# A four-block transformer on one core: head sums of the first attention as products of high and low parts

## The chip, the core and the metric

One core of a Trainium2 chip runs the whole network. The metric is the device time of one execution in microseconds. TensorE multiplies, VectorE, ScalarE and GpSimd work elementwise, SyncE issues the transfers. Each engine runs its own instructions in order; semaphores order them across engines.

## The reference

The input is x, 16 sequences of 256 tokens of 128 features. Four blocks follow, each with a residual: a gated linear attention, an expert FFN, a softmax attention, the FFN again. The change lies in the first:

```python
# phi_q, phi_k: elu(rope(.)) + 1; beta: decay; mix: softmax over the M = 2 memories; 32 heads, D = 4
K = K * bt[..., None] + pk[:, :, None, :]
S = S * bt[..., None, None] + pk[:, :, None, :, None] * vt[:, :, None, None, :]
num = jnp.einsum('bhd,bhmdc->bhmc', pq, S)
den = jnp.einsum('bhd,bhmd->bhm', pq, K) + EPS
y = jnp.sum(num / den[..., None] * mt[..., None], axis=2)
```

For each memory m, head and value component c (0 to 3), num is the sum over d of pq[d] · S[m][d, c].

## The kernel before, in words

The tokens are worked in NT = 8 tiles of 512 (two sequences), features on the partitions. `S[:, m, c, :]` holds, for memory m, 128 rows (d, head) by 512 tokens; c = 4 is the denominator. VectorE makes these ten rows per tile with scans (`scan`, L1619), then multiplies those of m = 0 with phi_q (`product`, L1626, in pieces of 512 and 1024 columns); GpSimd multiplies those of m = 1 (`product`, L755, five of 512 columns). TensorE sums over d with 128 × 128 tables of ones and zeros (`numerator`, L1171), four products in full precision (F32) per m, accumulating in bank 7 or 6; the four denominator sums are in `denominators` (L1181). VectorE makes the weights (L1694 to L1701), TensorE spreads them (`weights`, L1192), ScalarE copies them (L963), VectorE multiplies them with the numerators (`weighted`, L1603), GpSimd adds the two memories (L780), and TensorE projects (`project_y`, L1199 and L1203) in the next tile's first step.

Elsewhere an f32 product is replaced by three of type F32R (`split_product`, L343 to L345), whose operands are a rounded high part, made by a copy into an F32R tile on ScalarE, and a low part, the difference, made by a subtraction.

The order is written by hand. Stage t runs `CH` = 32 steps c. In each step of a stage with an FFN tile beside it (f = t − 2, so stages 2 to 9) stands one FFN unit: on TensorE gate, up and down, three products each; on ScalarE silu (L542) and the high part of the hidden row before (L552); on VectorE the gating product (L582), which reads PSUM, and, in odd steps, the low part (L558); on GpSimd the low part (L558) in even steps. TensorE's up of unit c waits for the L582 of unit c − 2 and its gate for silu of c − 2; down of c − 3 waits for that unit's low part. Behind the unit, each engine's `attn(t, c)` issues what of the attention belongs to step c. In stages 0 and 1 no FFN stands beside, and only the waits set the pace. Stage 2 also makes the high and low parts of all FFN weights: L466 on ScalarE, L471 on GpSimd. In stage t, steps 11 to 16 hold key products (L1609) and the scans of m = 0; 17 and 19 VectorE's products; 18 and 20 to 23 the scans of m = 1; 19 and 21 to 24 GpSimd's products; 20 and 22 the numerators of m = 0; 24 and 25 those of m = 1; 24 and 25 the weights; 28 and 29 the weighted products; 30 their sum.

After the first ten stages come the second attention and the second FFN.

Of the kernel before, what the change touches and what calls it, by code (L numbers as in the profile page):

```python
# [16 lines left out]
F32 = mybir.dt.float32  # L17
# [126 lines left out]
def program(nc, a_x, a_Wq, a_Wk, a_Wv, a_Wbeta, a_bbeta, a_Wmix, a_bmix, a_Wout, a_bout, a_ln_g, a_ln_b,  # L144
            b_Wq, b_bq, b_Wk, b_bk, b_Wv, b_bv, b_Wo, b_bo, f_Wg, f_Wu, f_Wd, consts, out):
    ctx = ExitStack()
    with ctx:  # L147
# [34 lines left out]
        ident = cst("ident")  # L182
        SELR = sb("SELR", [P, 2 * NJ + 3, P], F32R)
        MASKB = sb("MASKB", [P, 3, P], BF16)
        ONES = sb("ONES", [P, P])
# [30 lines left out]
        ARENA = sb("ARENA", [P, 20736])  # L216
        ARENA_R = sb("ARENA_R", [P, 20224], F32R)
        at = {F32: 0, F32R: 0}

        def take(*shape, dt=F32):  # L220
# [64 lines left out]
        XAH = take(TOK, dt=F32R)  # L285
        XAL = take(TOK, dt=F32R)
        at[F32R] = 0

# [15 lines left out]
        ld = sems("ld", "x0 x1 x tables_a tables_b wa wb ba bb")  # L304
        pr = sems("prep", "wt wtc la ones selr wb wout ba bmix bqkr bqk zero")
# [3 lines left out]
        A = sems("a", "u_k u_q ex_k ex_q re_k re_q phi_k phi_q clip scaled beta scan prod0 prod1 num0 num1 den dp rc "  # L309
                      "wgt rep rs ay y z zsum zg zb done")  # L310
# [4 lines left out]
        BPROJ = ["q", "qs", "k", "ks"]  # L315
        b_ready = {n: sem(f"b_{n}_ready") for n in BPROJ}
        b_used = {n: sem(f"b_{n}_used") for n in BPROJ}
        B = sems("b", "u_q u_k hi lo v_ready v_used st_ready st_used kst_ready kst_used row_ready row_used nmh nml "
# [88 lines left out]

        def f_source(n):
# [316 lines left out]
        def _(g):  # L725
# [31 lines left out]
            def attn(t, c):  # L757
                old, nxt = t - 1, t + 1
                if is_tile(t):
# [171 lines left out]
        def _(act):  # L931
# [22 lines left out]
            def half_tanh(t, m):  # L954
# [186 lines left out]
        def _(pe):  # L1141
# [65 lines left out]
            def attn(t, c):  # L1207
# [61 lines left out]
                if is_tile(t):  # L1269
                    if c == 20:  # L1270
                        pe.wait_ge(a_used["v3"], t + 1)
                        numerator(t, 0, (0, 1))
                    if c == 22:
                        numerator(t, 0, (2, 3))
                        pe.wait_ge(a_used["v2"], t + 1)
                        denominators(t)
                    if c == 24:
                        pe.wait_ge(n_a.lo, min(t + 2, NT))
                        after(pe, n_f.lo, t)
                        numerator(t, 1, (0, 1))  # L1280
                    if c == 25:
                        numerator(t, 1, (2, 3))
                    if c == 26:
                        weights(t, 0)
                    if c == 27:
                        weights(t, 1)
# [3 lines left out]
            def project_b(nxt, i):  # L1290

                pe.wait_ge(n_b.lo, NT + nxt.n + 1)
                if i:
                    pe.wait_ge(b_used[BPROJ[i - 1]], nxt.n + 1)
                split_product(pe, bank[6], WBH[:, i, :], WBL[:, i, :], XH[:, :],
                              XL[:, :]).then_inc(b_ready[BPROJ[i]], 1)

            def project_v(nxt, subs):

                pe.wait_ge(b_used[BPROJ[-1]], nxt.n + 1)  # L1300
                if 0 in subs:
# [52 lines left out]
            pe.wait_ge(pr.bqkr, 5)  # L1354
            pe.wait_ge(pr.selr, 1)
            pe.wait_ge(pr.ba, 2)
            for t in range(-1, NT + 2):
# [104 lines left out]
            def slot(t, b):  # L1462
# [3 lines left out]
                for k in range(UNITS):  # L1466
# [16 lines left out]
                    if k == T_LAG - 1 and has1:  # L1483
# [3 lines left out]
                        if b == 1 and nxt.real():  # L1487
                            pe.wait_ge(b_used[BPROJ[-1]], nxt.n + 1)
                        stack2(n - 1, op, 1 - b, 0)
# [55 lines left out]
        def _(v):  # L1545
# [83 lines left out]
            def attn(t, c):  # L1629
# [56 lines left out]
                if is_tile(t):  # L1686
# [10 lines left out]
                    if c == 25:  # L1697
# [3 lines left out]
                        v.scalar_tensor_tensor(WGT[:, :], MIX[:, :], 1.0, RC[:, :], ALU.add,  # L1701
                                               ALU.mult).then_inc(A.wgt, 1)
                    if c == 28:
                        weighted(t, 0)
                    if c == 29:
                        weighted(t, 1)

            def rope_b(t, k, name, table, dst, bias):
                v.wait_ge(b_ready[name], t.n + 1)
                after(v, (B.u_q, B.u_k)[k], t.n)  # L1710
                v.scalar_tensor_tensor(seqs(dst), seqs(bank[6]), bias, spread(cst(table), SPT), ALU.add,
                                       ALU.mult).then_inc(b_used[name], 1)

# [193 lines left out]
```

## Time and profile before

| | us |
|---|---|
| median of 3 runs | 1718.75 (1716.77 to 1719.26) |
| the profiled execution | 1717.04 |
| its span | 1715.2 |
| busy: TensorE / VectorE / ScalarE / GpSimd | 1613.6 / 1075.4 / 1014.2 / 888.1 |

A busy time says how much an engine did in the whole span, not where it set the pace, and it holds the time in which an instruction that has started is held up inside. A timeline row is one instruction or a few merged ones with start and duration; the idle time before it and what ended that stand in brackets. A matmul row's duration holds its pipeline's depth; the distance from start to start is what TensorE spends on it. A full-precision product leaves two records.

### The profile page before, as it was taken

To read this page: it belongs to the slowest core of one execution; us is meant where nothing else is said; L and a number is where in the kernel's file an instruction comes from. 1 tells how busy PE (TensorE), PEld (TensorE's weight loads), DVE (VectorE), ACT (ScalarE), POOL (GpSimd) and SP (SyncE) were. 2 spreads that over 40 slices of the span, in tenths; PEclk is the share of its full clock that TensorE was granted. 3 is DMA by queue.
4 is the path that set the end of the run, shared out by engine and by line. 5 is a ranking of instruction groups with operands and counts; after the bars stand their busy time and mean duration, and the time that the engine had idled before them with its cause. 6 is when DMAs were issued, how large, how long until landed. Compare 5 with 4: busy or idle time off the path is not lost. (4 is left out here: it accounts for less than half of the span.)

```text
span 1715.2 us, 24775 instructions
## 1 busy us (share of the span) xinstructions
PE 1613.6 (94%) x7232; PEld 1247.1 (73%) x7232; DVE 1075.4 (63%) x1871; ACT 1014.2 (59%) x1872; POOL 888.1 (52%) x793
## 2 busy tenths in 40 slices
PE   3678999999999999999999999988999999999998
PEld 2356677878787878886666666656888888888887
DVE  5667778686869595557666666643454554554544
ACT  2237464646464646555887878875555555555554
POOL 3669764646454544362777777773333333333322
PEclk9789999999999999999999999998999999999999
DMA  3035543444443435541000000012555555555554
GB/s 106 1 111 184 189 138 132 143 142 148 148 148 128 148 130 184 205 177 57 1 1 1 2 0 1 1 38 99 187 193 203 201 187 190 197 193 205 194 187 135
DMA packets 72548, 215.88 MB, mean 126 GB/s; under 512 B 7387, under 2 KB 20832, under 8 KB 72416
## 3 DMA queue, kind: packets, MB, share of 16 engines
q1 hardware_dynamic: 72416, 214.35, 36.1%
q8 instruction: 55, 0.90, 0.2%
q14 instruction: 77, 0.63, 0.1%
HBM read 199.64 MB, written 14.68 MB: 125 GB/s over the span
## 5 line engine op out<-in xcount | busy, mean ns | idle before, releaser
L558 POOL TENSOR_TENSOR ARENA_R<-ARENA,ARENA_R 128x512 fp32r<-128x512 f32 x256 | 344.1, 1344 | 600.3 <-ACT ARENA_R L552 599.5
L582 DVE TENSOR_TENSOR ARENA<-ARENA,pair 128x512 f32<-128x512 f32 x512 | 349.1, 682 | 449.0 <-PE pair L345 410.4
L542 ACT ACTIVATE ARENA<-bank 128x512 f32<-128x512 f32 x512 | 306.1, 598 | 464.8 <-PE bank L345 463.0
L343 PE MATMUL pair<-ARENA_R 128*128 128x512 f32 x1064 | 417.1, 392 | 10.6 <-DVE ARENA L582 5.0
L345 PE MATMUL pair<-ARENA_R 128*128 128x512 f32 x1064 | 414.7, 390 | 0.0
L344 PE MATMUL pair<-ARENA_R 128*128 128x512 f32 x1064 | 414.2, 389 | 0.0
L552 ACT ACTIVATE ARENA_R<-ARENA 128x512 fp32r<-128x512 f32 x512 | 319.9, 625 | 36.1 <-DVE ARENA L582 33.6
L913 POOL TENSOR_TENSOR ARENA_R<-ARENA,ARENA_R 128x512 fp32r<-128x512 f32 x192 | 249.2, 1312 | 80.0 <-ACT ARENA L1120 76.6
L343 PE MATMUL bank<-ARENA_R 128*128 128x512 f32 x568 | 239.8, 422 | 23.0 <-DVE ARENA L1609 17.7
L343 PEld LDWEIGHTS pair<-ARENA_R 128*128 128x128 f32 x1064 | 200.7, 189 | 60.2 <-issue 7.3
L345 PEld LDWEIGHTS pair<-ARENA_R 128*128 128x128 f32 x1064 | 200.8, 189 | 42.4
L344 PEld LDWEIGHTS pair<-ARENA_R 128*128 128x128 f32 x1064 | 200.9, 189 | 41.3
L344 PE MATMUL bank<-ARENA_R 128*128 128x512 f32 x568 | 223.6, 394 | 0.0
L345 PE MATMUL bank<-ARENA_R 128*128 128x512 f32 x568 | 223.5, 393 | 0.0
L558 DVE TENSOR_TENSOR ARENA_R<-ARENA,ARENA_R 128x512 fp32r<-128x512 f32 x256 | 195.4, 763 | 0.1
L1781 DVE TENSOR_REDUCE ARENA<-bank 128x2 f32<-128x512 f32 (+1 forms) x192 | 130.8, 688 | 76.2 <-PE bank L1379 43.8
L343 PEld LDWEIGHTS bank<-ARENA_R 128*128 128x128 f32 x568 | 108.1, 190 | 52.0 <-DVE ARENA L1609 21.4
L1415 PE MATMUL pair<-ARENA_R 128*128 128x512 f32 x384 | 135.2, 433 | 8.5 <-ACT ARENA L1096 6.9
L1120 ACT ACTIVATE ARENA_R<-pair 128x512 fp32r<-128x512 f32 x192 | 115.8, 603 | 34.0 <-PE pair L1403 25.7
L344 PEld LDWEIGHTS bank<-ARENA_R 128*128 128x128 f32 x568 | 108.3, 191 | 23.5 <-issue 4.3
L345 PEld LDWEIGHTS bank<-ARENA_R 128*128 128x128 f32 x568 | 107.9, 190 | 23.3
L1619 DVE TENSOR_TENSOR_SCAN ARENA<-ARENA 128x512 f32<-128x512 f32 x80 | 121.4, 1525 | 0.0
(216 smaller groups left out, 2027.1 us busy)
## 6 DMA issues: line engine op xcount, KB each, us to landing
ARENA_R<-split_weights SPq DMA_DIRECT2D x360, 512.0 KB, 4.7
split_weights<-ARENA_R SPq DMA_DIRECT2D x24, 512.0 KB, 3.9
X<-in_L_attn_a_x_dram SPq DMA_DIRECT2D x8, 256.0 KB, 5.4
ARENA<-in_L_ffn_Wg_dram SPq DMA_DIRECT2D x8, 256.0 KB, 2.9
ARENA<-in_L_ffn_Wu_dram SPq DMA_DIRECT2D x8, 256.0 KB, 3.4
ARENA<-in_L_ffn_Wd_dram SPq DMA_DIRECT2D x8, 256.0 KB, 3.9
out_dram<-X SPq DMA_DIRECT2D x8, 256.0 KB, 4.2
CST<-in_tables_dram SPq DMA_DIRECT2D x1, 835.5 KB, 4.6
```

What stands on the lines that cost most here:

```text
L343: pe.matmul(dst, wh, xh, start=start, stop=False)
L344: pe.matmul(dst, wh, xl, start=False, stop=False)
L345: return pe.matmul(dst, wl, xh, start=False, stop=stop)
L542: act.activation(SG[:, c % 2, :], bank[c % 2], ACT.Silu).then_inc(F.sil, 1)
L552: act.activation(HH[:, G % FC, :], HF[:, G % FC, :], ACT.Copy).then_inc(F.hh, 1)
L558: eng.tensor_tensor(HL[:, G % FC, :], HF[:, G % FC, :], HH[:, G % FC, :].bitcast(F32), ALU.subtract).then_inc(lo_done(G)[0], 1)
L582: v.tensor_tensor(HF[:, c % FC, :], SG[:, c % 2, :], bank[2 + c % 2], ALU.mult).then_inc(F.mul, 1)
L913: g.tensor_tensor(PL[:, u % RING, :], PT[:, u % RING, :], PH[:, u % RING, :].bitcast(F32), ALU.subtract).then_inc(B.pl, 1)
L1120: act.activation(dst[:, u % RING, :], bank[2 + u % 2], ACT.Exp, scale=DB ** -0.5).then_inc(B.t_used, 1)
L1415: m = pe.matmul(bank[4 + qb], VS[:, p, 2 * ob + kb, at:at + P], (PH, PL)[i][:, u % RING, :], start=(u < 2 and i == 0), stop=(g == NG - 1 a ...
L1619: v.tensor_tensor_scan(S[:, m, c, :], BETA[:, m, :], KV[:, c, :], 0.0, ALU.mult, ALU.add).then_inc(A.scan, 1)
L1781: v.tensor_reduce(dst, src, AX.X, ALU.max, negate=True).then_inc(B.row_used, 1)
```

## The change

The four products per m of `numerator` become eight: each `S[:, m, c, :]` is split into a high part `NUH` (ScalarE, two components at once) and a low part `NUL` (for m = 0 on GpSimd, for m = 1 on VectorE), and both are multiplied with a rounded copy `SUMR` of the sum tables, which GpSimd makes at the start. Steps move: numerators to 21 and 23 (m = 0), 26 and 28 (m = 1), the second weighted product to 30, the sum to 31. The eight semaphores of the second attention's four projections become two counters, `b_ready` and `b_used`; the waits name the same events. The core of the diff:

```diff
         ARENA_R = sb("ARENA_R", [P, 20480], F32R)        # was 20224
+        NUH = take(2, 2, TOK, dt=F32R)
+        NUL = take(2, 2, TOK, dt=F32R)
...
+        def product_lo(eng, t, m, p):
+            eng.wait_ge(A.nuh, 4 * t + 2 * m + p + 1)
+            if m == 0:
+                after(eng, A.num1, t)
+            else:
+                eng.wait_ge(A.num0, t + 1)
+            for i in range(2):
+                eng.tensor_tensor(NUL[:, p, i, :], S[:, m, 2 * p + i, :], NUH[:, p, i, :].bitcast(F32),
+                                  ALU.subtract).then_inc(A.nul, 1)
...  GpSimd, start
+            g.wait_ge(ld.tables_a, 16)
+            for c in range(DA):
+                g.tensor_copy(SUMR[:, c, :], cst(f"sum_{c}")).then_inc(pr.sumr, 1)
             a_rstd(g, 0)
...  GpSimd, step
                     if c in (19, 21, 22, 23, 24):
                         product(t, (19, 21, 22, 23, 24).index(c))
-                    if c == 30:
+                    if c in (19, 21):
+                        product_lo(g, t, 0, (c - 19) // 2)
+                    if c == 31:
                         g.wait_ge(A.ay, 2 * (t + 1))
...
             def rotated(nxt, i):
                 name = "qk"[i]
-                after(g, b_used[name], nxt.n + 1)
-                after(g, b_used[name + "s"], nxt.n + 1)
+                after(g, *projected(b_used, nxt, name + "s"))
...  ScalarE
+            def product_hi(t, m, p):
+                if m == 0:
+                    act.wait_ge(A.prod0, 3 * t + 2 + p)
+                    after(act, A.num1, t)
+                else:
+                    act.wait_ge(A.prod1, 5 * t + 3 + 2 * p)
+                    act.wait_ge(A.num0, t + 1)
+                act.activation(NUH[:, p, :, :], S[:, m, 2 * p:2 * p + 2, :], ACT.Copy).then_inc(A.nuh, 1)
...
+                    if c in (18, 20):
+                        product_hi(t, 0, (c - 18) // 2)
+                    if c in (24, 26):
+                        product_hi(t, 1, (c - 24) // 2)
...  TensorE
-            def numerator(t, m, comps):
-                for c in comps:
-                    pe.wait_ge(*((A.prod0, 3 * t + 2 + c // 2) if m == 0 else (A.prod1, 5 * t + 2 + c)))
-                    x = pe.matmul(bank[(7, 6)[m]], cst(f"sum_{c}"), S[:, m, c, :], start=(c == 0), stop=(c == DA - 1))
-                if DA - 1 in comps:
+            def numerator(t, m, p):
+                pe.wait_ge(A.nul, 8 * t + 4 * m + 2 * p + 2)
+                for i in range(2):
+                    for part in (NUH, NUL):
+                        x = pe.matmul(bank[(7, 6)[m]], SUMR[:, 2 * p + i, :], part[:, p, i, :],
+                                      start=(p + i == 0 and part is NUH), stop=(p + i == 2 and part is NUL))
+                if p:
                     x.then_inc((A.num0, A.num1)[m], 1)
...  steps: numerator(t, 0, 0) at c == 21, (t, 0, 1) at 23, (t, 1, 0) at 26 ahead of weights(t, 0), (t, 1, 1) at 28
...  VectorE
+                    if c == 25:
+                        product_lo(v, t, 1, 0)
+                    if c == 27:
+                        product_lo(v, t, 1, 1)
                     if c == 28:
                         weighted(t, 0)
-                    if c == 29:
+                    if c == 30:
                         weighted(t, 1)
```

## Rows read from the trace of the kernel before

**Rows 1.** The page: busy us, share of the span and instructions of each engine.
```profile
PE 1613.6 (94%) x7232; PEld 1247.1 (73%) x7232; DVE 1075.4 (63%) x1871; ACT 1014.2 (59%) x1872; POOL 888.1 (52%) x793
```

**Rows 2.** Four stretches: busy us (instructions) by engine, clock, DMA.
```profile
core 0: us, PE busy (x) PEld busy (x) DVE busy (x) ACT busy (x) POOL busy (x), PEclk, DMA share, GB/s
42.00:62.00 20.00, 14.88 (x35) 7.30 (x36) 14.48 (x13) 1.19 (x2) 12.15 (x6) 0.82 0.00 1
172.00:200.00 28.00, 25.60 (x95) 17.61 (x96) 25.19 (x23) 12.98 (x24) 24.24 (x15) 1.00 0.45 158
329.20:375.10 45.90, 44.16 (x183) 33.24 (x182) 45.83 (x58) 24.38 (x46) 24.09 (x21) 1.00 0.41 138
375.40:390.50 15.10, 14.79 (x66) 11.96 (x65) 7.87 (x12) 8.10 (x15) 5.11 (x4) 1.00 0.47 164
```

**Rows 3.** VectorE's timeline: start, duration; in brackets idle time and releaser.
```profile
329.18 0.69 DVE L582 TENSOR_TENSOR ARENA<-ARENA,pair 128x512 f32<-128x512 f32 x1 [4.57 <-ACT ARENA L542]
375.40 0.69 DVE L582 TENSOR_TENSOR ARENA<-ARENA,pair 128x512 f32<-128x512 f32 x1 [0.29 <-PE pair L345]
...
641.86 0.69 DVE L582 TENSOR_TENSOR ARENA<-ARENA,pair 128x512 f32<-128x512 f32 x1 [0.28 <-PE pair L345]
```

**Rows 4.** TensorE's timeline, steps 20 and 26 of tile 4.
```profile
353.38 0.47 PE L343 MATMUL pair<-ARENA_R 128*128 128x512 f32 x1 [0.47 <-DVE ARENA L582]
...
375.88 1.02 PE L1192 MATMUL pair<-ARENA,CST 128*128 128x256 f32 x4
```

**Rows 5.** VectorE's timeline in steps 17 to 21 of tile 4.
```profile
349.73 2.92 DVE L1626 TENSOR_TENSOR ARENA<-ARENA 128x512 f32<-128x512 f32 x2
...
354.30 0.66 DVE L582 TENSOR_TENSOR ARENA<-ARENA,pair 128x512 f32<-128x512 f32 x1
354.87 1.41 DVE L558 TENSOR_TENSOR ARENA_R<-ARENA,ARENA_R 128x512 fp32r<-128x512 f32 x1
356.20 2.30 DVE L1626 TENSOR_TENSOR ARENA<-ARENA 128x1024 f32<-128x1024 f32 x1
...
359.02 1.21 DVE L1619 TENSOR_TENSOR_SCAN ARENA<-ARENA 128x512 f32<-128x512 f32 x1
...
362.07 2.28 DVE L1619 TENSOR_TENSOR_SCAN ARENA<-ARENA 128x512 f32<-128x512 f32 x1
```

**Rows 6.** GpSimd's timeline in steps 19, 20 and 24.
```profile
354.45 1.28 POOL L755 TENSOR_TENSOR ARENA<-ARENA 128x512 f32<-128x512 f32 x1 [2.90 <-DVE ARENA L1619]
355.69 1.73 POOL L558 TENSOR_TENSOR ARENA_R<-ARENA,ARENA_R 128x512 fp32r<-128x512 f32 x1
...
371.01 1.29 POOL L755 TENSOR_TENSOR ARENA<-ARENA 128x512 f32<-128x512 f32 x1 [1.16 <-DVE ARENA L1619]
```

**Rows 7.** L558 by line (min/median/max ns), and L1626 in tile 0.
```profile
L558 DVE TENSOR_TENSOR ARENA_R<-ARENA,ARENA_R x256: 675/685/1458, 116.9 to 1707.3; 128x512 fp32r<-128x512 f32 x128
...
43.84 1.20 DVE L1626 TENSOR_TENSOR ARENA<-ARENA 128x1024 f32<-128x1024 f32 x1
```

**Rows 8.** TensorE's timeline around the first numerator of tile 4.
```profile
354.85 1.88 PE L1171 MATMUL bank<-ARENA,CST 128*128 128x512 f32 x4
...
356.80 0.40 PE L344 MATMUL bank<-ARENA_R 128*128 128x512 f32 x1
```

**Rows 9.** Lines by form: ScalarE's copies of 1024 columns.
```profile
L1035 ACT ACTIVATE ARENA_R<-CST 128x1024 fp32r<-128x1024 f32 x2 | 2.1, 1050 | 0.0
```

**Rows 10.** Timeline of tile 0: GpSimd's products, VectorE's second weighted product.
```profile
44.01 10.89 POOL L755 TENSOR_TENSOR ARENA<-ARENA 128x512 f32<-128x512 f32 x5 [10.86 <-DVE ARENA L1619]
...
59.42 0.69 DVE L1603 TENSOR_TENSOR ARENA<-ARENA,bank 128x512 f32<-128x512 f32 x1 [1.13 <-ACT ARENA L963]
```

**Rows 11.** Timeline of the start, and GpSimd's copies by form.
```profile
8.60 0.69 PE L1151 MATMUL bank<-CST,ARENA 128*128 128x128 f32 x2 [8.60 <-DMA CST<-in_tables_dram]
...
10.74 0.23 POOL L368 TENSOR_SCALAR VE<-MV 128x4 f32<-128x4 f32 x1 [9.28 <-DVE MV L360]
...
L823 POOL CAST SELR<-ARENA 128x128 fp32r<-128x128 f32 x4 | 1.2, 293 | 0.0
```

More of the change, by code:

```diff
@@ L183, in program @@
         SELR = sb("SELR", [P, 2 * NJ + 3, P], F32R)
+        SUMR = sb("SUMR", [P, DA, P], F32R)
         MASKB = sb("MASKB", [P, 3, P], BF16)
@@ L216, in program @@
         ARENA = sb("ARENA", [P, 20736])
-        ARENA_R = sb("ARENA_R", [P, 20224], F32R)
+        ARENA_R = sb("ARENA_R", [P, 20480], F32R)
         at = {F32: 0, F32R: 0}
@@ L304, in program @@
         ld = sems("ld", "x0 x1 x tables_a tables_b wa wb ba bb")
-        pr = sems("prep", "wt wtc la ones selr wb wout ba bmix bqkr bqk zero")
+        pr = sems("prep", "wt wtc la ones selr wb wout ba bmix bqkr bqk zero sumr")
         PROJ = ["k", "ks", "b0", "b1", "q", "qs", "mx", "v0", "v1", "v2", "v3"]
@@ L308, in program @@
         a_used = {n: sem(f"a_{n}_used") for n in PROJ}
-        A = sems("a", "u_k u_q ex_k ex_q re_k re_q phi_k phi_q clip scaled beta scan prod0 prod1 num0 num1 den dp rc "
+        A = sems("a", "u_k u_q ex_k ex_q re_k re_q phi_k phi_q clip scaled beta scan prod0 prod1 nuh nul num0 num1 den dp rc "
                       "wgt rep rs ay y z zsum zg zb done")
@@ L315, in program, with projected @@
         BPROJ = ["q", "qs", "k", "ks"]
-        b_ready = {n: sem(f"b_{n}_ready") for n in BPROJ}
-        b_used = {n: sem(f"b_{n}_used") for n in BPROJ}
+        b_ready, b_used = sem("b_proj_ready"), sem("b_proj_used")
+        def projected(sm, t, name):
+            return sm, len(BPROJ) * t.n + BPROJ.index(name) + 1
         B = sems("b", "u_q u_k hi lo v_ready v_used st_ready st_used kst_ready kst_used row_ready row_used nmh nml "
@@ L1269, in attn @@
                 if is_tile(t):
-                    if c == 20:
+                    if c == 21:
                         pe.wait_ge(a_used["v3"], t + 1)
-                        numerator(t, 0, (0, 1))
+                        numerator(t, 0, 0)
                     if c == 22:
-                        numerator(t, 0, (2, 3))
                         pe.wait_ge(a_used["v2"], t + 1)
                         denominators(t)
-                    if c == 24:
+                    if c == 23:
+                        numerator(t, 0, 1)
+                    if c == 26:
                         pe.wait_ge(n_a.lo, min(t + 2, NT))
                         after(pe, n_f.lo, t)
[L1280 to L1283, printed above, removed]
+                        numerator(t, 1, 0)
                         weights(t, 0)
+                    if c == 28:
+                        numerator(t, 1, 1)
                     if c == 27:
@@ L1293, in project_b @@
                 if i:
-                    pe.wait_ge(b_used[BPROJ[i - 1]], nxt.n + 1)
+                    pe.wait_ge(*projected(b_used, nxt, BPROJ[i - 1]))
                 split_product(pe, bank[6], WBH[:, i, :], WBL[:, i, :], XH[:, :],
-                              XL[:, :]).then_inc(b_ready[BPROJ[i]], 1)
+                              XL[:, :]).then_inc(b_ready, 1)
             def project_v(nxt, subs):
-                pe.wait_ge(b_used[BPROJ[-1]], nxt.n + 1)
+                pe.wait_ge(*projected(b_used, nxt, BPROJ[-1]))
                 if 0 in subs:
@@ L1355, in _ @@
             pe.wait_ge(pr.selr, 1)
+            pe.wait_ge(pr.sumr, DA)
             pe.wait_ge(pr.ba, 2)
@@ L1487, in slot @@
                         if b == 1 and nxt.real():
-                            pe.wait_ge(b_used[BPROJ[-1]], nxt.n + 1)
+                            pe.wait_ge(*projected(b_used, nxt, BPROJ[-1]))
                         stack2(n - 1, op, 1 - b, 0)
@@ L1702, in attn @@
                                                ALU.mult).then_inc(A.wgt, 1)
+                    if c == 25:
+                        product_lo(v, t, 1, 0)
+                    if c == 27:
+                        product_lo(v, t, 1, 1)
                     if c == 28:
                         weighted(t, 0)
-                    if c == 29:
+                    if c == 30:
                         weighted(t, 1)
             def rope_b(t, k, name, table, dst, bias):
-                v.wait_ge(b_ready[name], t.n + 1)
+                v.wait_ge(*projected(b_ready, t, name))
                 after(v, (B.u_q, B.u_k)[k], t.n)
                 v.scalar_tensor_tensor(seqs(dst), seqs(bank[6]), bias, spread(cst(table), SPT), ALU.add,
-                                       ALU.mult).then_inc(b_used[name], 1)
+                                       ALU.mult).then_inc(b_used, 1)
             def split_b(nxt, i):
```

## The prediction

> **What bounds the kernel now.** I read the page first: TensorE is busy 94% of the span [rows 1], which invites a sum made on TensorE alone. So I next took the stretches of the first 650 us, where the first attention runs, and then each engine's own timeline in one of them. From tile 3 on the stages are copies of each other, 88.8 us apart: the L582 of step c = 26 starts at 375.40 in tile 4 and at 641.86 in tile 7, three stages on [rows 3]. I work in tile 4. From its step c = 9 (329.2) to c = 26 (375.1) TensorE is busy 44.16 of 45.90 us, but VectorE is busy 45.83 of 45.90 [rows 2]: after it waited 4.57 us for ScalarE at 329.18 it does not stand idle until 375.40, and then only 0.29 us [rows 3]. Two engines are full there. TensorE may run two FFN units ahead of VectorE's gating product L582 and no further; at 353.38 it hit that limit [rows 4]. After c = 26 TensorE alone is full: 14.79 of 15.10 us, VectorE 7.87 [rows 2].
>
> VectorE is full partly with waiting. Its products with two SBUF inputs and GpSimd's take turns. L755 on GpSimd starts at 354.45 and ends at 355.73; VectorE's L558 starts at 354.87 and takes 1.41 instead of its usual 0.68, so it ends 0.6 after GpSimd does. GpSimd's next one starts at 355.69 and takes 1.73 instead of 1.28; VectorE's L1626 of 1024 columns starts at 356.20 and takes 2.30 instead of 1.20; the scan at 362.07 takes 2.28, the one at 359.02 takes 1.21 [rows 5 to 7]. The L582 at 354.30, which reads PSUM, keeps its 0.66 under the same GpSimd product. As pitches (start to start, since neighbours overlap by some 0.08) I use: GpSimd product 1.25, VectorE product 0.60, scan 1.13, L1626 1.13, PSUM product 0.58.
>
> The rule for this stands in the Trainium skill, SBUF — State Buffer, section "Who interferes with whom": a VectorE instruction with two SBUF inputs and a GpSimd one that reads SBUF exclude each other, and whichever issues second is blocked until the first ends; a VectorE instruction with at most one SBUF input is free. The trace agrees (1.41 against 0.68, and 0.66). It speaks against this change; were PSUM readers blocked too, the stage sum below would be some 1.2 higher.
>
> **The change, part by part.**
>
> TensorE. A full-precision product of 512 columns: two of them (four records) start at 354.85, the next L344 at 356.80, its L343 one pitch of 0.23 before; (1.95 − 0.23)/2 = 0.86 each [rows 8]. A product of rounded parts takes the pitch of 0.228. Per tile 8 × 0.86 = 6.9 go and 16 × 0.228 = 3.65 come: −3.2 us of TensorE work. For eight tiles that would be −26, if TensorE set the time everywhere.
>
> ScalarE: four copies of 1024 columns, 1.05 each, the duration of a copy of that size [rows 9]. ScalarE is busy 24 of 46 us, so the work itself fits. The first stands before silu of c = 19 and waits for VectorE's product, which ends at 352.65 [rows 5]; it ends at 353.7 and silu at 354.3, just when L582 of c = 19 began: nothing lost. Behind the others the next silu comes in time too (worked below).
>
> GpSimd: four subtractions of 512 columns, all at c = 19 and 21, that is inside the full stretch. VectorE: four, at c = 25 and 27, 0.60 pitch each. These I follow through the stretch by the turns above. At c = 19 GpSimd: product to 355.7 as before, low part 1 after L558, 356.2 to 357.4; VectorE L1626 to 358.5; low part 2 in a gap where GpSimd stood idle before, 358.5 to 359.75. The scan of c = 20, ready at 359.0, is held until 359.75 and ends 360.9 (before 360.2). GpSimd's hidden low part (L558) of unit 19 now comes third, to 362.1; so L558 of VectorE in c = 21 ends 362.75, GpSimd's product 364.0, the scan of c = 21 at 365.1, L582 of c = 22 starts at 365.7, some 0.8 later than before. Low parts 3 and 4 take 365.1 to 366.4 and 367.5 to 368.8 and, with the operations queued behind them, put L582 of c = 24 at 371.8 and of c = 25 at 374.55, each 1.0 later than before. GpSimd's last product slips from 371.01 to 376.2 [rows 5, 6]; VectorE's L558 and weight product of c = 25 take turns with GpSimd's delayed L558 and last product and end at 377.8 (before, by the 0.29 of idle time ahead of 375.40, at 375.1); the two new subtractions of c = 25 end at 379.0. The inputs are ready: ScalarE's third copy waits for a product that ends at 373.05. So L582 of c = 26 starts at 379.0 instead of 375.40: +3.6, of which 1.2 is the new work and 2.4 to 2.7 turns lost to GpSimd. TensorE's 46 us shrink to about 41 there and hide under it: its saving is worth nothing in this stretch, since VectorE was the full one already.
>
> From c = 26 on TensorE sets the pace. Before, weights(0) started at 375.88 [rows 4]. Now four products of the second numerator (0.91) wait for VectorE's subtractions at 379.05 and stand ahead of it, so it starts at 379.96: +4.1. Four more come in c = 28: +5.0 at c = 29, and there it stays. The later slots of the second weighted product (c = 30) and of the sum (c = 31) cost nothing: from its L582, 0.6 + 0.6 + 1.3 against 4.8 us of TensorE work that still precede the output projection. Per tile of this kind +5.0; bounds: +2.3 if all four GpSimd subtractions fall beside work that does not exclude them (then weights(0) starts at 375.1 + 1.2 + 0.9 = 377.2, +1.4, and 0.9 follow), +7.8 if all 5.0 us of them are added and a wait on ScalarE with them. I take 5.0, by the turns. Five such tiles (3 to 7): +25.
>
> Tile 2 also splits the FFN weights; GpSimd is busy 24.24 and VectorE 25.19 of 28 us there [rows 2], GpSimd with hardly a gap. Here the full 5.0 counts, plus 1.2 and the tail less TensorE's waits for GpSimd that exist already: +7 (4 to 9).
>
> Tiles 0 and 1 have no FFN beside them; latency decides. In tile 0 GpSimd's five products (44.01 to 54.89) and VectorE's scans take turns without a hole [rows 10]; four more of 1.25 put the last product's end at 60.0. Then copy 1.05, subtraction 1.25, numerator about 1: the second weighted product, at 59.42 before, starts near 64, +4.5; in tile 1 +4.3 (the end of its chain releases the weight split that the FFN's first unit waits for). Bounds 2 to 6 each.
>
> The four copies of the sum tables at the start cost 0.29 each [rows 11], from 8.6 (TensorE's first use of the tables) to 9.8; GpSimd idles until 10.74. Nothing; 0.5 if the tables land late for it. The merged semaphores of the second attention name the same last events: nothing.
>
> **Sum.** 25 + 7 + 4.5 + 4.3 = +40.8. The profiled execution took 1717.04 (its span 1715.2 and 1.8 around it), 1.7 below the median: 1757.8, or 1759.5 with the median's offset. I say 1758. The bounds together: 5 × 2.3 + 4 + 4 = +19.5 and 5 × 7.8 + 9 + 12 = +60.
>
> **The rivals.**
> (A) TensorE sets the time, VectorE's fill being elastic (much of it is waiting for GpSimd, and would shift to better places): the saving counts in six tiles, −19, the first two lose 2 to 4 together: about 1700. For it: TensorE 94% busy, its tail stretch full. Against: VectorE has 0.07 us without work in 45.9 [rows 2], and the change adds to it. It decides if the new L582 of c = 26 comes no later after c = 9 than before. Chance 0.11.
> (B) Gain and loss cancel: turns cost little and TensorE gives 1 us per tile back: 1714 to 1722. 0.05.
> (C) GpSimd's subtractions mostly fit; only the new VectorE work and the tail remain: +5 to +18, 1722 to 1735. For it: GpSimd had holes of 2.90 us in front of its products [rows 6]. Against: in those holes VectorE runs operations that exclude it. 0.12.
> (D) Heavier than the sum: TensorE, now with gaps of 2 to 3 us in the stretch, is granted a lower clock. In tile 0 the granted clock is 0.82 with TensorE busy 14.88 of 20 us [rows 2]; in the stretch it would be busy 41 of 50. Had it half its rate in the stretch it would need far more than VectorE: +60 and beyond. Against: the stretch from 172 to 200, with 2.4 of its 28 us idle, keeps 1.00. 0.05.
> The forecast itself, +19.5 to +60: 0.67, with 1744 to 1774 as its own likely range.
>
> **Numbers.** What this kernel's measurement can tell from no change is 0.2%, 3.4 us. Faster by more: A and a little of B, 0.12. Within: 0.05, most of B and the edge of C. Slower by more: 0.83. The range 1724 to 1784 leaves out A and B and part of D: below 2 in 10.
>
> **What would show it.** In the changed trace: stages of the fourth tile and later 93.8 us apart instead of 88.8 (A: 85.6); VectorE still without idle time from c = 9 to c = 26, and that stretch near 50 us; more of VectorE's scans and L558 blocked to 2.3 and 1.4; TensorE idle several us in the stretch, waiting for VectorE or GpSimd; numerators of 16 short products; the first tile's second weighted product near 64. Wrong if VectorE shows gaps in the stretch or if GpSimd's subtractions take their 1.28 while VectorE's neighbours keep 0.68 and 1.21.

## The result, and the profile after

| | before | after |
|---|---|---|
| median | 1718.75 us | 1778.95 us (1777.89 to 1780.73, 4 runs) |
| ratio in runs taken side by side | 1 | 1.0351, 95% interval 1.0335 to 1.0368 |
| the profiled execution, its span | 1717.04, 1715.2 | 1777.89, 1776.1 |

The change makes the kernel 60 us slower; +41 was forecast. Line numbers moved: L582 is L599, L558 L575, L1619 L1657, L1626 L1664, L755 L775, L1171 L1207, L1181 L1218, L1192 L1229, L1603 L1641, L542 L559, L963 L994, L343 to L345 L349 to L351; the subtractions are L422 on both engines, ScalarE's copies L989.

The page of the changed kernel, busy time by engine, answers to [rows 1]:
```profile
PE 1610.3 (91%) x7232; PEld 1258.2 (71%) x7232; DVE 1111.2 (63%) x1903; ACT 1043.0 (59%) x1904; POOL 955.4 (54%) x829
```
TensorE is busy only 3.3 us less, not 26. Its attention lines, grouped, before and then after (instructions, busy, mean ns):
```profile
L1171 PE MATMUL bank<-ARENA,CST 128*128 128x512 f32 x128 | 66.9, 648 | 12.8 <-DVE ARENA L1626 9.3 <-POOL ARENA L755 3.3
L1192 PE MATMUL pair<-ARENA,CST 128*128 128x256 f32 x64 | 17.3, 392 | 3.7 <-ACT ARENA L963 3.7
```
```profile
L1207 PE MATMUL bank<-ARENA_R,SUMR 128*128 128x512 f32 x128 | 48.0, 509 | 70.7 <-POOL ARENA_R L422 43.1 <-DVE ARENA_R L422 27.6
L1229 PE MATMUL pair<-ARENA,CST 128*128 128x256 f32 x64 | 25.3, 537 | 3.8 <-ACT ARENA L994 3.8
```
The numerators save 18.9 us of records; the weights, the same 64 instructions, take 8.0 more, and TensorE stands 70.7 us in front of the numerators instead of 12.8. GpSimd has 67 us more from 36 more instructions; its 32 subtractions account for 60 (a group by line and form: busy, mean ns):
```profile
L422 POOL TENSOR_TENSOR ARENA_R<-ARENA,ARENA_R 128x512 fp32r<-128x512 f32 x32 | 60.3, 1905 | 0.0
L422 DVE TENSOR_TENSOR ARENA_R<-ARENA,ARENA_R 128x512 fp32r<-128x512 f32 x32 | 25.8, 849 | 0.0
```
1905 ns each where 1.25 us is a GpSimd product's pitch: the rest is waiting inside, for VectorE.

Where the 61 us of span sit I read from one marker, the L599 of step c = 9 of each stage (VectorE waits 4.57 us for ScalarE there, in tile 2 about 5.0). The distances from one marker to the next:

| part | before | after | added | forecast |
|---|---|---|---|---|
| start to tile 2's marker (tiles 0, 1) | 140.22 | 158.90 | 18.7 | 8.8 |
| tile 2's marker to tile 3's | 100.1 | 109.9 | 9.7 | 7 |
| tile 3's to tile 7's, each | 88.8 | 95.2 | 6.4 | 5.0 |
| tile 7's to the end | 1119.6 | 1126.4 | 6.9 | 5.0 |

Each distance is read from one execution. Ahead of tile 2's marker the run with fillers from tile 2 on (below) has the code of the changed kernel, and there that marker stands at 159.86 instead of 158.90: a difference of 1 us in tiles 0 and 1 means nothing.

Four stretches of the changed kernel, the last two against [rows 2]; the first two are of tiles 0 and 1 (the kernel before's row of 42 to 60 us stands below, in the run of TensorE's saving alone):
```profile
core 0: us, PE busy (x) PEld busy (x) DVE busy (x) ACT busy (x) POOL busy (x), PEclk, DMA share, GB/s
42.00:60.00 18.00, 5.71 (x16) 4.14 (x16) 14.19 (x12) 4.12 (x5) 15.80 (x9) 0.64 0.00 0
110.00:128.00 18.00, 12.21 (x30) 8.20 (x29) 8.96 (x10) 5.43 (x8) 8.96 (x8) 0.63 0.00 0
363.70:413.10 49.40, 41.11 (x178) 31.89 (x177) 49.26 (x60) 28.68 (x51) 35.03 (x26) 1.00 0.41 139
418.40:434.50 16.10, 15.76 (x74) 12.88 (x73) 8.61 (x13) 7.28 (x14) 5.13 (x4) 1.00 0.46 164
```
In tile 4's stretch VectorE has again no idle time and TensorE has 8.3 us of it, as forecast. VectorE's timeline, the L599 of c = 9, 26 and 27 (start, duration):
```profile
363.77 0.69 DVE L599 TENSOR_TENSOR ARENA<-ARENA,pair 128x512 f32<-128x512 f32 x1 [4.57 <-ACT ARENA L559]
...
413.15 0.67 DVE L599 TENSOR_TENSOR ARENA<-ARENA,pair 128x512 f32<-128x512 f32 x1
418.45 0.69 DVE L599 TENSOR_TENSOR ARENA<-ARENA,pair 128x512 f32<-128x512 f32 x1 [4.62 <-PE pair L351]
```
From c = 9 to c = 26 it is 49.38 us instead of 46.22 [rows 3]: +3.2, where +3.6 was forecast. The turns stand in the two timelines, GpSimd's first:
```profile
390.29 3.96 POOL L422 TENSOR_TENSOR ARENA_R<-ARENA,ARENA_R 128x512 fp32r<-128x512 f32 x2
394.22 2.20 POOL L575 TENSOR_TENSOR ARENA_R<-ARENA,ARENA_R 128x512 fp32r<-128x512 f32 x1
...
398.07 3.47 POOL L422 TENSOR_TENSOR ARENA_R<-ARENA,ARENA_R 128x512 fp32r<-128x512 f32 x2
```
```profile
390.82 2.30 DVE L1664 TENSOR_TENSOR ARENA<-ARENA 128x1024 f32<-128x1024 f32 x1
393.04 0.67 DVE L599 TENSOR_TENSOR ARENA<-ARENA,pair 128x512 f32<-128x512 f32 x1
393.64 1.70 DVE L1657 TENSOR_TENSOR_SCAN ARENA<-ARENA 128x512 f32<-128x512 f32 x1
...
396.89 2.30 DVE L1657 TENSOR_TENSOR_SCAN ARENA<-ARENA 128x512 f32<-128x512 f32 x1
...
400.29 2.33 DVE L1657 TENSOR_TENSOR_SCAN ARENA<-ARENA 128x512 f32<-128x512 f32 x1
```
Scans that take 1.21 alone take 1.70 to 2.33 here, beside GpSimd's subtractions and the operations queued behind them; the L599 at 393.04, which reads PSUM, keeps its 0.67. The rest of the stage's loss, 3.3 us, comes after c = 26. TensorE's timeline there, against 375.88 of [rows 4]:
```profile
394.40 1.16 PE L1207 MATMUL bank<-ARENA_R,SUMR 128*128 128x512 f32 x4 [2.48 <-POOL ARENA_R L422]
...
413.38 2.01 PE L1207 MATMUL bank<-ARENA_R,SUMR 128*128 128x512 f32 x4 [3.54 <-DVE ARENA_R L422]
415.18 1.84 PE L1229 MATMUL pair<-ARENA,CST 128*128 128x256 f32 x4
```
Two things show. The weights stand behind a numerator piece that waits 3.54 us for VectorE. And after that wait both run at half rate: the four short products and the weights take 2.01 and 1.84 us in all, where the weights before took 1.02 and the equal piece at 394.40, after a wait of 2.48, took 1.16. The granted clock says the same; it was 1.00 up to 413.10 and is 1.00 again from 418.40 on, but not between:
```profile
413.40:416.80 3.40, 3.40 (x9) 2.76 (x9) 0.43 (x1) 0.00 (x0) 0.00 (x0) 0.50 0.00 0
```
The kernel before has 1.00 from tile 3's marker to tile 7's.

Tile 0's timeline of TensorE, against [rows 10]:
```profile
51.35 2.04 PE L1207 MATMUL bank<-ARENA_R,SUMR 128*128 128x512 f32 x4 [15.60 <-POOL ARENA_R L422]
53.20 2.79 PE L1218 MATMUL pair<-ARENA,CST 128*128 128x256 f32 x8
...
61.14 1.45 PE L1207 MATMUL bank<-ARENA_R,SUMR 128*128 128x512 f32 x4 [4.07 <-DVE ARENA_R L422]
62.38 1.91 PE L1229 MATMUL pair<-ARENA,CST 128*128 128x256 f32 x4
64.98 2.07 PE L1229 MATMUL pair<-ARENA,CST 128*128 128x256 f32 x4 [0.69 <-ACT ARENA L994]
66.49 2.27 PE L1207 MATMUL bank<-ARENA_R,SUMR 128*128 128x512 f32 x4
```
GpSimd's last product ends at 59.50 (60.0 was forecast), but the second weighted product starts at 68.86, not near 64.

### The profile page after: what moved, and what is told of

Read it like the earlier page. It is cut to its first block and busy times, and to the rows that moved or that the text cites. A ratio compares the mean times of both kernels' runs of the same rounds, so it can differ in the third digit from the quotient of the medians.

```text
span 1776.1 us, 24933 instructions
## 1 busy us (share of the span) xinstructions
PE 1610.3 (91%) x7232; PEld 1258.2 (71%) x7232; DVE 1111.2 (63%) x1903; ACT 1043.0 (59%) x1904; POOL 955.4 (54%) x829
## 5 line engine op out<-in xcount | busy, mean ns | idle before, releaser
L575 POOL TENSOR_TENSOR ARENA_R<-ARENA,ARENA_R 128x512 fp32r<-128x512 f32 x256 | 346.5, 1354 | 616.2 <-ACT ARENA_R L569 616.1
L599 DVE TENSOR_TENSOR ARENA<-ARENA,pair 128x512 f32<-128x512 f32 x512 | 349.4, 683 | 463.5 <-PE pair L351 424.8
L559 ACT ACTIVATE ARENA<-bank 128x512 f32<-128x512 f32 x512 | 306.1, 598 | 471.0 <-PE bank L351 469.4
L349 PE MATMUL pair<-ARENA_R 128*128 128x512 f32 x1064 | 418.5, 393 | 15.6 <-POOL ARENA_R L488 7.1
L351 PE MATMUL pair<-ARENA_R 128*128 128x512 f32 x1064 | 415.1, 390 | 0.0
L349 PE MATMUL bank<-ARENA_R 128*128 128x512 f32 x568 | 233.6, 411 | 23.2 <-DVE ARENA L1647 18.4
L349 PEld LDWEIGHTS pair<-ARENA_R 128*128 128x128 f32 x1064 | 201.1, 189 | 68.8 <-POOL ARENA_R L488 9.7
L351 PEld LDWEIGHTS pair<-ARENA_R 128*128 128x128 f32 x1064 | 201.2, 189 | 42.4
L351 PE MATMUL bank<-ARENA_R 128*128 128x512 f32 x568 | 223.2, 393 | 0.0
L575 DVE TENSOR_TENSOR ARENA_R<-ARENA,ARENA_R 128x512 fp32r<-128x512 f32 x256 | 193.9, 758 | 0.1
L349 PEld LDWEIGHTS bank<-ARENA_R 128*128 128x128 f32 x568 | 108.6, 191 | 49.3 <-DVE ARENA L1647 21.8
L1657 DVE TENSOR_TENSOR_SCAN ARENA<-ARENA 128x512 f32<-128x512 f32 x80 | 127.6, 1602 | 0.0
L351 PEld LDWEIGHTS bank<-ARENA_R 128*128 128x128 f32 x568 | 108.0, 190 | 23.4
```

Source lines behind the costliest of these rows:

```text
L349: pe.matmul(dst, wh, xh, start=start, stop=False)
L351: return pe.matmul(dst, wl, xh, start=False, stop=stop)
L559: act.activation(SG[:, c % 2, :], bank[c % 2], ACT.Silu).then_inc(F.sil, 1)
L575: eng.tensor_tensor(HL[:, G % FC, :], HF[:, G % FC, :], HH[:, G % FC, :].bitcast(F32), ALU.subtract).then_inc(lo_done(G)[0], 1)
L599: v.tensor_tensor(HF[:, c % FC, :], SG[:, c % 2, :], bank[2 + c % 2], ALU.mult).then_inc(F.mul, 1)
L1657: v.tensor_tensor_scan(S[:, m, c, :], BETA[:, m, :], KV[:, c, :], 0.0, ALU.mult, ALU.add).then_inc(A.scan, 1)
```

## The experiments

**GpSimd's subtractions alone.** The kernel before, with four more GpSimd subtractions per tile that read constants and that nobody waits for.
```diff
+                    if c in (19, 21):
+                        p = (c - 19) // 2
+                        for i in range(2):
+                            g.tensor_tensor(NUL[:, p, i, :], CST[:, 0:TOK], CST[:, P:P + TOK], ALU.subtract)
```


> The kernel before, with four more subtractions of 512 columns on GpSimd per tile, at c = 19 and 21 where the change puts its low parts, and two inputs in SBUF like those; they subtract constants and nobody reads or waits for them, so nothing else of the change is in it. Theory 1 (GpSimd and VectorE take turns): VectorE's stretch from c = 9 to c = 26 grows by 2.4 to 2.7 us in tiles 3 to 7, tile 2 by some 4, tiles 0 and 1 by 4 to 5 each since GpSimd's last product comes 5 us later: +25, 1739 to 1748. Rival (VectorE's fill is elastic, GpSimd's work fits into its gaps): under +5, and the extra time of the change sits elsewhere.

Measured: 1752.19 us, ratio 1.0199 (1.0182 to 1.0216), above the 1748 of the forecast. Stages 91.4 apart, +2.6, inside the 2.4 to 2.7 of the forecast; tiles 0 and 1 together +14.2, more than expected; tile 2 +5.4. From tile 3's marker to tile 7's the granted clock is 1.00, so the 2.6 hold nothing of TensorE's clock. GpSimd's timeline of tile 4:
```profile
377.90 3.97 POOL L781 TENSOR_TENSOR ARENA_R<-CST 128x512 fp32r<-128x512 f32 x2
381.82 2.18 POOL L559 TENSOR_TENSOR ARENA_R<-ARENA,ARENA_R 128x512 fp32r<-128x512 f32 x1
```
The subtractions have no dependency with any VectorE instruction and still take 1.98 each: what couples the two engines is not data. GpSimd's slack doesn't absorb them.

**VectorE's subtractions alone.** The kernel before, with two VectorE subtractions of constants at c = 25 and two at c = 27.
```diff
+                    if c in (25, 27):
+                        p = (c - 25) // 2
+                        for i in range(2):
+                            v.tensor_tensor(NUL[:, p, i, :], CST[:, 0:TOK], CST[:, P:P + TOK], ALU.subtract)
```


> The kernel before, with four more subtractions of 512 columns on VectorE per tile, two at c = 25 and two at c = 27, of constants, with no reader. Theory 1: the two at c = 25 stand in the full stretch, 0.60 each, 1.2 per tile in six tiles; those at c = 27 stand in VectorE's idle time; tiles 0 and 1 hide all: +7, 1724 to 1728. Rival (elastic): within 2 us of the kernel before.

Measured: 1718.38 us, ratio 1.0002 (0.9992 to 1.0012). A miss for my theory: VectorE, full without a hole, took 1.2 us of work at c = 25 for nothing. VectorE's timeline shows how it is made up:
```profile
375.48 1.29 DVE L1707 TENSOR_TENSOR ARENA_R<-CST 128x512 fp32r<-128x512 f32 x2
376.68 0.68 DVE L583 TENSOR_TENSOR ARENA<-ARENA,pair 128x512 f32<-128x512 f32 x1
378.75 0.69 DVE L583 TENSOR_TENSOR ARENA<-ARENA,pair 128x512 f32<-128x512 f32 x1 [1.39 <-PE pair L346]
```
c = 26 is late by some 0.8 us (marker at 329.62), but TensorE's own queue holds two units before it needs that product, and by c = 27 VectorE waits for TensorE again, on time: the L583 of c = 27 starts 49.13 us after the marker, the kernel before's L582 (378.32) 49.14.

**TensorE's saving alone.** The kernel before, its numerators without components 1 and 3 (these are missing from the output): 3.4 us per tile less for TensorE, every wait kept.
```diff
-                    x = pe.matmul(...)
+                    if c in (0, 2):
+                        x = pe.matmul(..., start=(c == 0), stop=(c == 2))
```


> The kernel before with components 1 and 3 of both numerators left out of the sums, all waits and all else kept: 3.4 us less TensorE work per tile in the same steps, about what the change saves, and nothing added. It prices the saving alone. Theory (VectorE is as full as TensorE from c = 9 to c = 26): weights(0) can start when VectorE has made the weight product, at 375.1 instead of 375.88, so 0.8 us in each of six tiles, and 1 to 2 in tiles 0 and 1: 1709 to 1714. Rival (TensorE alone sets the time; the run with more VectorE work cost nothing): 3.4 in each of six tiles and 1 to 2 in the others, 1694 to 1698.

Measured: 1717.86 us, ratio 1.0003 (0.9992 to 1.0014), outside both forecasts. Stages 0.5 shorter (88.28), tile 2 0.9 shorter, tiles 0 and 1 2.7 longer. TensorE, 94% busy, gives 0.5 of its 3.4 us per stage back, and over the whole kernel nothing. The stretch from 42 to 60 us of tile 0, in the kernel before and then here:
```profile
42.00:60.00 18.00, 14.38 (x32) 6.84 (x32) 14.38 (x13) 1.19 (x2) 10.89 (x5) 0.80 0.00 1
```
```profile
42.00:60.00 18.00, 12.57 (x24) 5.75 (x24) 13.78 (x12) 0.66 (x2) 10.88 (x5) 0.69 0.00 0
```
With 1.8 us less TensorE work the granted clock is 0.69 instead of 0.80, and the tile got later: its second weighted product starts at 60.57 instead of 59.42.

**TensorE kept busy before c = 26.** The changed kernel, with 14 short products that nobody needs issued ahead of the wait, in tiles 2 to 7.
```diff
+                        if t >= 2:
+                            for _ in range(14):
+                                pe.matmul(bank[6], SUMR[:, 0, :], SUMR[:, :, :], start=True, stop=True)
                         numerator(t, 1, 0)
```


> The changed kernel, with 14 products that nobody needs (3.2 us at full rate) on TensorE in tiles 2 to 7, ahead of the wait for VectorE's low parts at c = 26, where its trace shows TensorE idle for 3.54 us and then eight products at half rate. Theory 2 (the clock is part of the loss): TensorE comes out of the wait at the full clock, the numerator pieces take 0.91 instead of 1.8 and the weights 0.67 instead of 1.35, some 1.8 us per tile: 11 us off, near 1768, although work is added. Rival (the slow products are caused by their operands arriving late, or only look slow): no change, or up to 2 us slower per tile where the added products outlast the wait.

Measured: 1769.28 us, ratio 1.0288 (1.0270 to 1.0305): 10 us faster than the changed kernel, by adding work. Stages 93.65 apart, 1.6 less. TensorE's timeline:
```profile
408.33 3.36 PE L1320 MATMUL bank<-SUMR 128*128 128x512 f32 x14
411.71 1.20 PE L1207 MATMUL bank<-ARENA_R,SUMR 128*128 128x512 f32 x4
412.74 1.02 PE L1229 MATMUL pair<-ARENA,CST 128*128 128x256 f32 x4
```
The piece and the weights are back at full rate: the half rate behind c = 26 came with TensorE's wait there. The low clock isn't gone, though. It now falls inside the stretch, behind the wait for GpSimd at c = 21 (these are the windows of tile 4's stretch and of the low clock in it):
```profile
362.20:411.58 49.38, 45.16 (x192) 35.81 (x190) 49.31 (x60) 28.59 (x51) 35.05 (x26) 0.97 0.42 139
393.80:397.20 3.40, 3.40 (x9) 2.67 (x8) 3.40 (x3) 1.12 (x2) 3.40 (x3) 0.50 0.00 0
```
There it costs nothing: the stretch lasts 49.38 us, as in the changed kernel, where it had 1.00. The same 3.4 us at half clock are dear where TensorE sets the pace and free where VectorE does. Behind tile 7's marker this trace has a granted clock of 0.53 from 868 to 879 us, which no run here explains; the distances used end before it.

**The same in tiles 0 and 1 as well**: 60 and 20 more ahead of the first numerator piece, 14 ahead of the third.
```diff
+                        if t < 2:
+                            for _ in range((60, 20)[t]):
+                                pe.matmul(bank[7], SUMR[:, 0, :], SUMR[:, :, :], start=True, stop=True)
                         numerator(t, 0, 0)
```


> The filled kernel again, with products that nobody needs in tiles 0 and 1 too: 60 and 20 ahead of the first numerator piece, 14 ahead of the third piece, all in time in which TensorE waits for GpSimd or VectorE. Theory 1 (half of the excess of tiles 0 and 1 is TensorE's clock: granted 0.64 from 42 to 60 us, first piece 2.04 instead of 1.15, denominators 2.99, the last piece 2.27, the weights 1.76 and 2.07): the denominators of tile 0 take about 1.9 again and the weights about 1.0, and tile 2's c = 9 comes 4 to 7 us earlier than in the kernel that is filled from tile 2 on (159.86): 153 to 156, the time 1762 to 1765. Rival 2 (the turns of VectorE and GpSimd and the order of TensorE's queue set tiles 0 and 1, its rate does not): products at full rate, but tile 2's c = 9 within 2 us of 159.9 and the time 1767 to 1771. Rival 3 (the fillers end too late and delay the first piece): later than 160.

Measured: 1763.87 us, ratio 1.0261 (1.0244 to 1.0278). Tile 2's marker at 155.65, 4.2 earlier than with fillers from tile 2 on and 3.2 earlier than in the changed kernel; the granted clock of 42 to 60 us is 0.92. TensorE's timeline of tile 0:
```profile
55.25 1.10 PE L1207 MATMUL bank<-ARENA_R,SUMR 128*128 128x512 f32 x4
56.19 1.89 PE L1218 MATMUL pair<-ARENA,CST 128*128 128x256 f32 x8
...
63.47 1.02 PE L1229 MATMUL pair<-ARENA,CST 128*128 128x256 f32 x4
65.18 1.13 PE L1229 MATMUL pair<-ARENA,CST 128*128 128x256 f32 x4 [0.69 <-ACT ARENA L994]
65.96 1.29 PE L1207 MATMUL bank<-ARENA_R,SUMR 128*128 128x512 f32 x4
```
The fillers ran too long and delayed the first piece: 51.35 in the changed kernel, 55.25 now, of which GpSimd explains 1.3 (the subtraction that the piece needs ended at 52.51, there at 51.21). The tile still ended earlier: its second weighted product starts at 67.35 instead of 68.86. So at least some 3 of the 18.7 us are the clock.

**Weights ahead of the second numerator.** The changed kernel; at c = 26 only `weights(t, 0)`, both pieces at c = 28.
```diff
                     if c == 26:
+                        weights(t, 0)
+                    if c == 28:
                         pe.wait_ge(n_a.lo, min(t + 2, NT))
                         after(pe, n_f.lo, t)
                         numerator(t, 1, 0)
-                        weights(t, 0)
-                    if c == 28:
                         numerator(t, 1, 1)
```


> The changed kernel with one thing in another order on TensorE: at c = 26 weights(0) alone, and both pieces of the second numerator at c = 28, so that the FFN units 27 and 28 no longer queue behind VectorE's low parts. Theory 3 (the order of TensorE's queue carries the part that the port does not): weights(0) starts at once after VectorE's weight product, 3 to 4 us earlier than in the changed kernel, in six tiles, and some 2 to 4 us in tiles 0 and 1: 22 to 28 us off, 1751 to 1757. What remains over the kernel before is then the longer stretch and 1.8 us of second numerator per tile. If the port alone were the cause (theory 1 alone): 5 us off or less.

Measured: 1754.87 us, ratio 1.0219 (1.0202 to 1.0237). Stages 92.4 apart, the last 92.8: 2.7 less in the mean; tiles 0 and 1 5.8 less. TensorE's timeline:
```profile
400.98 1.13 PE L1229 MATMUL pair<-ARENA,CST 128*128 128x256 f32 x4 [2.11 <-DVE ARENA L1739]
...
407.56 2.03 PE L1207 MATMUL bank<-ARENA_R,SUMR 128*128 128x512 f32 x8
```
The numerator waits for nothing at c = 28, and the weights for 2.11 us. All of them run at full rate; here too a half rate stands in the stretch, behind the wait at c = 21.

**No low parts on GpSimd.** The changed kernel; for m = 0 the high part is multiplied twice (its low part is missing).
```diff
-                    if c in (19, 21):
-                        product_lo(g, t, 0, (c - 19) // 2)
...
-                pe.wait_ge(A.nul, 8 * t + 4 * m + 2 * p + 2)
+                if m == 0:
+                    pe.wait_ge(A.nuh, 4 * t + p + 1)
+                else:
+                    pe.wait_ge(A.nul, 4 * t + 2 * p + 2)
...
-                    for part in (NUH, NUL):
+                    for part, src in ((NUH, NUH), (NUL, NUL if m else NUH)):
```


> The changed kernel without GpSimd's four subtractions per tile: for m = 0 the high part is multiplied twice, so TensorE, ScalarE and VectorE keep their work, and the low part of m = 0 is missing from the result. Theory (turns at the port): the 2.6 us per stage that four such subtractions added to the kernel before come off here, and in tiles 0 and 1 some 7 each, with TensorE's wait for them: 34 to 42 off, 1737 to 1745. Rival (in the changed kernel the loss is in TensorE's queue and the clock at c = 26, and stays when GpSimd is relieved): 1765 or more.

Measured: 1762.21 us, ratio 1.0261 (1.0241 to 1.0282): a miss. Tiles 0 and 1 gain 11.8, but a stage only 1.0 to 1.7 (93.9 in the mean), and tile 2 only 1.0. Stages of 94.2 and of 93.6 alternate with the clock: 0.96 and 0.98. TensorE's timeline of tile 4 (marker at 350.11):
```profile
397.95 1.91 PE L1208 MATMUL bank<-ARENA_R,SUMR 128*128 128x512 f32 x4 [4.29 <-DVE ARENA_R L422]
399.66 1.91 PE L1230 MATMUL pair<-ARENA,CST 128*128 128x256 f32 x4
```
The stretch is 1.8 shorter (47.6 against 49.4), but the wait at c = 26 is still there, now 4.29, and the half rate with it.

**Both edits together.** The last two diffs, weights first and no low parts on GpSimd, in one kernel.

> The changed kernel with both edits at once: GpSimd's four low parts left out (the low part of memory 0 is missing; its high part is multiplied twice), and the first weight product ahead of the second numerator, both pieces of which stand at c = 28. Alone, the first took 1.1 to 1.7 us off a stage and 11.8 off tiles 0 and 1, the second 2.9 off a stage and 5.8 off all before tile 2's c = 9. Theory 1 (with GpSimd's low parts gone, the tail at c = 26 took over what they gave; with the tail gone too, each stage loses 2.9 and the 2.4 to 2.7 of the turns): stages 89.8 to 90.4, the time 1728 to 1735. Rival 2 (the two overlap; what the turns cost does not come back): stages 91 to 92.4, 1740 to 1750.

Measured: 1736.08 us, ratio 1.0098 (1.0082 to 1.0115), a touch above theory 1's end; stages 90.1 to 91.0 apart, 90.45 in the mean, tile 2's marker at 146.08. Against the same order with GpSimd's subtractions (92.5 in the mean), the turns cost 2.0 per stage; against the kernel without them but in the old order (93.9), the order gives 3.4. Alone the two edits gave 1.3 and 2.7, together 4.8: neither takes the other's gain. The stages differ with the clock here too: the two of 90.1 have a granted clock of 1.00, those of 90.6 and 91.0 have 0.98.

**Denominators ahead too.** The kernel with the weights first, and `denominators` at c = 20 instead of 22, ahead of the first piece.
```diff
+                    if c == 20:
+                        pe.wait_ge(a_used["v2"], t + 1)
+                        denominators(t)
                     if c == 21:
...
-                    if c == 22:
-                        pe.wait_ge(a_used["v2"], t + 1)
-                        denominators(t)
```


> The kernel of the run with the weights first, and in addition the denominators at c = 20, ahead of the first piece of the first numerator, which waits for GpSimd. In the changed kernel's tile 0 VectorE idles 3.74 us for the denominators that stand behind that piece. Theory (that order costs where no FFN runs beside): 1 to 3 us in each of tiles 0 and 1, nothing in the others: 1749 to 1753. Rival (VectorE's later work hides it): as the run with the weights first, 1755.

Measured: 1759.6 us, ratio 1.0246 (1.0225 to 1.0267), slower than without this edit. Tiles 0 and 1 gain the 1.8 that was expected, tile 2 loses 3.7 and tile 3 1.3, later stages are equal; behind tile 7's marker the profiled execution has another 2.7, far from this edit. In tile 2 TensorE now stops at the denominators:
```profile
189.39 2.68 PE L1218 MATMUL pair<-ARENA,CST 128*128 128x256 f32 x8 [2.81 <-POOL ARENA L775]
```
They wait for GpSimd's first product, the denominators' own, with an FFN unit queued behind them. I count that as the likely cause; no run isolates it.

**Only the second memory in parts.** m = 0 as before the change; m = 1 split, its numerator at c = 28; no low parts on GpSimd.
```diff
-                    if c == 21:
+                    if c == 20:
                         pe.wait_ge(a_used["v3"], t + 1)
-                        numerator(t, 0, 0)
+                        full_numerator(t, (0, 1))
                     if c == 22:
+                        full_numerator(t, (2, 3))
...
-                    if c == 23:
-                        numerator(t, 0, 1)
```


> Only m = 1 in parts: m = 0 is summed in full precision at c = 20 and 22 as before the change, GpSimd makes no low part; ScalarE's and VectorE's parts of m = 1 stay, and both pieces of that numerator stand at c = 28 behind the weights. TensorE does 1.6 us less per tile, but 1.8 of its work moves from the full stretch into the part that TensorE bounds. Theory (VectorE full): +1.8 less the 0.8 that weights(0) gains, 1.0 in six tiles, and 2 to 3 in tiles 0 and 1: 1727 to 1731. Rival (TensorE's total counts): 1.6 off in six tiles, 1709 to 1714.

Measured: 1737.61 us, ratio 1.0111 (1.0094 to 1.0128), 6 us above expectation; stages 90.6 to 91.5 (90.6 at a granted clock of 1.00, 91.2 and 91.5 at 0.98), tiles 0 and 1 +6.4. Even with no GpSimd work added and its numerator behind the weights the split costs 1.8 to 2.7 per stage. No version tried beats the kernel before.

## Why the prediction was right, and where its sizes were off

**Direction and mechanism held, the size only just.** The time is inside the stated 1724 to 1784, but outside the likely 1744 to 1774, and the 61 us of added span lie just above the +60 to which the sum's own bounds reached: three of its terms were too small. TensorE's saving is worth almost nothing in the stretch: shown, 0.5 of 3.4 us per stage with the products left out. That rules out rival A, for which TensorE sets the time. The turns with GpSimd cost 2.6 per stage by themselves, against 2.4 to 2.7 forecast; taken out of the changed kernel they give back 1.8 in the stretch and 1.3 in the stage, and 2.0 with the weights first. Rival C (they fit) falls. The stretch grew by 3.2, forecast 3.6. What the Trainium skill says under SBUF — State Buffer, "Who interferes with whom" held in the changed kernel too: instructions with two SBUF inputs were held up (scans 1.70 to 2.33), the PSUM reader was not (0.67).

**The tail term of tiles 3 to 7 was too small.** The "four products of the second numerator (0.91)" and four more at c = 28 were to add 1.4 to the stretch's 3.6; the tail added 3.3. The sum took every short product at 0.228. After the 3.54 us wait that this sum itself put in front of them, they and the weights ran at half that rate: 1.6 us per stage, shown by the fillers. That is rival D's mechanism, which I had only asked about inside the stretch and not behind the one long wait that the change adds. In the changed kernel tile 4's stretch kept 1.00, as D's counter-row said; with the fillers and with the weights first it did not, and the stretch was no longer for it (49.38 and 49.31). Without the wait, in the order with the weights first, 2.7 per stage go, this 1.6 among them.

**The 1.2 us of VectorE work were argued wrongly.** I let them count because VectorE was full. Alone they cost nothing: TensorE has two units in hand at c = 26. In the change VectorE's lag counts because a TensorE instruction at c = 26 waits for VectorE's very last work, and everything behind it in the queue waits along; the order with the weights first bears this out, though it doesn't price the 1.2 by themselves. The stretch's own number (+3.2 for +3.6) isn't at fault, for VectorE's work alone made c = 26 late by 0.8 too; that such a lag reaches the next stage was right here for a reason that I hadn't given, and so by luck. What remains without the wait and GpSimd's part is 1.65 per stage (90.45 − 88.8), 1.3 in the two stages at full clock; which of VectorE's subtractions, ScalarE's copies, the eight additional short products behind c = 26 and the later slots make that up, no run separates.

**Tiles 0 and 1 are the largest error**: 18.7 for 8.8, where the bounds ended at 12. The step "latency decides" followed only GpSimd's products to 60.0, and they came at 59.50; what was behind them was priced at the old rates. Three parts are shown. GpSimd's eight subtractions (10.0 us at 1.25 each) delay VectorE's and TensorE's chains by more than their own length: alone +14.2, without them −11.8. The clock is in the +14.2 too, since in that run 42 to 60 us has 0.69. TensorE, with 5.71 us of work in 18 instead of 14.38, has a clock of 0.64 instead of 0.80: at least some 3. The queue order, denominators behind the first piece and weights behind the third: 5.8 with the weights moved and 1.8 with the denominators. These parts overlap (the clock and the order share the third piece's wait) and don't add up to 18.7.

**Tile 2**: +9.7 for 7, over its bound of 9. GpSimd's subtractions alone add 5.4 there, but taken out of the changed kernel they give back only 1.0, so its parts stay open.

## What to carry to other kernels

That an engine is busy without a hole doesn't make it critical, nor does 94%: ask which instruction of another engine waits for its last piece of work, and how much that engine has in hand. Put a new wait behind the queued work that doesn't need it; 2.7 of 6.4 us per stage were that, the clock's share in it. Price a product behind a long wait of TensorE at both rates that traces show after such waits, and ask whether TensorE or another engine sets the pace there: 3.4 us at half clock cost 1.6 us per stage behind c = 26 and nothing in the stretch. Take work off TensorE in a latency-bound stage only after a look at its clock.

## What the runs showed that I had not expected

- 14 unneeded products of 512 columns before a wait made the kernel 10 us faster in six tiles; with 108 more in the first two, where TensorE idled 16 us, another 5.4.
- Half of TensorE's numerator work left out lowered the granted clock of tile 0 from 0.80 to 0.69 and made tiles 0 and 1 2.7 us longer.
- The fillers of tiles 2 to 7 didn't remove the low clock of tile 4's stage but moved it: it starts 31.6 us after the marker (393.8) instead of 49.6 (413.4), out of the part in which TensorE sets the pace.
- A wait of 2.48 us on GpSimd was followed by full rate in one kernel (1.16 for four products at 394.40) and by half rate in another (2.05 at 383.35 in the kernel with the weights first), though TensorE was busy 13.4 of the 13.9 us ahead of the wait in both. With the fillers from tile 2 on, a wait of 2.49 was followed by 1 us at full rate and then by the half rate. One wait's length doesn't tell which of the two levels, 2.4 or 1.2 GHz, follows.
- Two GpSimd subtractions of constants took 3.97 us (1.98 each, where a GpSimd product's pitch is 1.25) beside VectorE's 1024-column product of 2.30.
